# Row-maximum stage of a causal attention layer: wider units, two-bank PSUM buffers and a lead of one unit

## The reference, cut to what matters

```python
x = L0_attn_x                      # (4, 2048, 256) fp32
xn = layernorm(x)
q, k, v = split(xn @ Wqkv.T)       # 16 heads of 16
dots = (q @ k.T) * 16 ** -0.5      # per batch and head, 2048 x 2048
dots = where(causal_mask, -inf, dots)
out = softmax(dots) @ v            # softmax(z) = exp(z - max z) / sum
attn = out @ Wout.T + bout
ffn = fp4_linear(silu(fp4_linear(xn, w_gate)) * fp4_linear(xn, w_up), w_down)
return x + attn + ffn
```

## Time and profile before

| | us |
|---|---|
| runs, median of 3 | 2633.95 (2632.21 to 2635.04) |
| profiled execution | 2634.47 |
| its span | 2632.8 |
| row-maximum stage in it | 254.5 to 962.4 |
| PE busy over the span | 2336.7 (89%) |
| DVE busy over the span | 1962.6 (75%) |
| ACT busy over the span | 1956.8 (74%) |

### The profile page before, as it was taken

How to read it: one execution, slowest core, us unless ns; L and a number is a source line. 1 busy time by engine, 2 the same in 40 slices (tenths; PEclk the granted TensorE clock), 3 DMA queues, 4 the chain that set the end, 5 groups by cost and what they waited for, 6 DMA issues and landing times.

```text
span 2632.8 us, 86210 instructions
## 1 busy us (share of the span) xinstructions
PE 2336.7 (89%) x34104; PEld 1294.7 (49%) x34104; DVE 1962.6 (75%) x5676; ACT 1956.8 (74%) x3342; POOL 918.4 (35%) x780
## 2 busy tenths in 40 slices
PE   2896999999999957999999989899998999989998
PEld 1784444444444424445455545455544455554455
DVE  6675999999999975766666667576676666667665
ACT  1343999999999956787777777777777777777775
POOL 3212233333333323333333333333333433334332
PEclk7898999999999988999999999999999999999999
DMA  2576445555555513101201101201011021011000
GB/s 62 176 225 146 69 72 73 73 72 72 73 72 73 72 28 75 28 12 33 61 19 42 38 17 30 60 23 36 22 39 28 13 66 40 19 38 30 13 20 30
DMA packets 94537, 143.82 MB, mean 55 GB/s; under 512 B 24896, under 2 KB 73920, under 8 KB 93632
## 3 DMA queue, kind: packets, MB, share of 16 engines
q1 hardware_dynamic: 89792, 129.50, 25.3%
q0 software_dynamic: 4352, 8.92, 1.4%
HBM read 104.20 MB, written 34.14 MB: 53 GB/s over the span
## 4 chain that ended last, share of the span: by engine, by line
PE 35%; DVE 11%; ACT 10%; issue 7%; DMA 0%; SPq 0%; POOL 0%; DVEq 0%; ACTq 0%; POOLq 0%
PE O L1052 10%; ACT probs L1180 8%; PE F L1073 7%; PE S L1031 6%; PE F L1110 6%; PE F L1119 2%; DVE silu L1376 2%; DVE o_turned L1409 1%; PE S L1037 1%; DVE o_packed L1421 1%; PE F L1099 1%; ACT ht_hi L1198 1%; DVE gated L1380 1%; DVE o_turned L1410 1%; DVE h_amax L1331 1%
## 5 line engine op out<-in xcount | busy, mean ns | idle before, releaser
L1180 ACT ACTIVATE probs<-S 128x1024 f32<-128x1024 f32 (+3 forms) x1280 | 1081.7, 899 | 381.2 <-PE S L1031 195.1
L775 ACT ACTIVATE m_excess<-m_DIFF 128x512 f32<-128x512 f32 (+7 forms) x1536 | 646.8, 472 | 85.0 <-PE m_DIFF L735 39.8
L793 DVE CUSTOM_DVE_ANT_0 m_excess<-m_S,m_excess 128x512 f32<-128x512 f32 (+7 forms) x1536 | 700.5, 530 | 11.1 <-PE m_S L735 9.4
L1052 PE MATMUL O<-probs,v_sb 64*32 64x512 f32 (+3 forms) x10240 | 615.9, 536 | 18.5 <-DVE o_turned L1410 15.8
L1031 PE MATMUL S<-q_st,k_st 64*32 64x512 f16 (+3 forms) x10240 | 440.7, 349 | 141.9 <-ACT probs L1180 99.9
L733 PE MATMUL m_S<-m_k,m_q 128*128 128x512 f16 (+7 forms) x1536 | 482.1, 324 | 26.7 <-DVE m_row_max L793 17.4
L733 PE MATMUL m_DIFF<-m_k,m_q_diff 128*128 128x512 f16 (+7 forms) x1536 | 476.9, 318 | 26.4 <-DMA m_q_diff<-s_q 26.1
L1031 PEld LDWEIGHTS S<-q_st,k_st 64*32 64x32 f16 x10240 | 170.3, 91 | 521.4 <-ACT probs L1180 356.0
L677 POOL TENSOR_TENSOR m_q_diff<-m_zero,m_q 48x4096 f16<-48x4096 f16 x32 | 224.4, 7011 | 428.0 <-DMA m_q<-s_q 417.3
L733 PEld LDWEIGHTS m_S<-m_k,m_q 128*128 128x128 f16 x1536 | 148.0, 96 | 276.7 <-DVE m_row_max L793 195.9
L735 PE MATMUL m_S<-m_future,m_ident 128*128 128x64 bf16 x1024 | 197.0, 193 | 0.0
(11 more groups left out here) (182 smaller groups left out, 4140.8 us busy)
## 6 DMA issues: line engine op xcount, KB each, us to landing
m_q<-s_q SPq DMA_DIRECT2D x96, 128.0 KB, 3.8
m_k<-s_k SPq DMA_DIRECT2D x96, 128.0 KB, 6.8
m_q_diff<-s_q SPq DMA_DIRECT2D x96, 128.0 KB, 8.1
k_st<-s_k SPq DMA_DIRECT2D x96, 128.0 KB, 4.4
q_st<-s_q SPq DMA_DIRECT2D x384, 32.0 KB
m_k<-s_k SPq DMA_DIRECT2D x96, 124.0 KB, 5.3
a_x<-in_L_attn_x_dram POOLq DMA_DIRECT2D x16, 512.0 KB, 4.8
s_q<-a_part SPq DMA_DIRECT2D x32, 256.0 KB, 2.4
```

Of the source, the lines that this page charges most:

```text
L775: act.activation(excess[u % MAX_EXCESS][:, 0:keys // 2], DIFF[u % MAX_BUFS][:, 0:keys // 2], ACT.Relu) \
L793: dve.tensor_tensor_reduce(larger, S[u % MAX_BUFS][:, 0:keys // 2], larger, 1.0, -3e38, ALU.add, ALU.max, column).then_inc(reduced[u % MAX ...
L1052: ins = pe.matmul(O[e][s * SLOT:(s + 1) * SLOT, st.skip:QC], v_sb[st.group % 2][rows, st.j, s * SLOT:(s + 1) * SLOT], probs[s // 2][st.n % ...
L1180: act.activation(probs[half][st.n % PROBS][:, :, 0:st.width], S[half][:, :, 0:st.width], ACT.Exp, scale=scale).then_inc(exped[half], 1)
```

## The change

Query blocks are no longer cut. A unit is a whole block with up to 1024 columns, 16 units to a head instead of 24. DIFF and S have two buffers each, of two banks (1024 columns). Blocks 8 to 15 ("wide") take a buffer; blocks 0 to 7 ("narrow") lie two to a buffer, one in each bank. The order of a head's blocks, with the buffer: 15 (0), 8 (1), 7 and 0 (0), 6 and 1 (1), 14 (0), 9 (1), 13 (0), 10 (1), 5 and 2 (0), 4 and 3 (1), 12 (0), 11 (1). PE writes a wide unit with two matmuls and the mask; the number of matmuls stays the same. The semaphores are one for each kind, and a unit waits for the last one that held any of its banks (`holders`). The lead of the differences is one unit instead of two. `excess` has six buffers of 1024 columns instead of eight of 512. `second_max` and the join at the end of a round are gone.

```diff
-MAX_KEYS = 1024
-MAX_BUFS = 4
-MAX_EXCESS = 8
-MAX_LEAD = 2
+MAX_COLS = T // 2
+MAX_HALF = MAX_COLS // 2
+MAX_EXCESS = 6
+MAX_LEAD = 1
...
+class MaxUnit:
+    def __init__(self, block, buf, at):
+        self.block, self.buf, self.at = block, buf, at
+        self.cols = (block + 1) * PAIR
+        self.banks = [(buf, b) for b in range(at // MAX_HALF, (at + self.cols - 1) // MAX_HALF + 1)]
...
+    wide = [(i, i - NKB // 2) for i in range(NKB - 1, NKB - NKB // 4 - 1, -1)]
+    wide = [(i, NKB + NKB // 2 - 1 - i) for i, _ in wide]
+    narrow = [(i, NKB // 2 - 1 - i) for i in range(NKB // 2 - 1, NKB // 4 - 1, -1)]
     units = []
+    for n, pair in enumerate(wide):
+        units += [MaxUnit(i, buf, 0) for buf, i in enumerate(pair)]
+        if n % 2 == 0:
+            units += [MaxUnit(i, buf, at) for buf in range(2) for at, i in zip((0, MAX_HALF), narrow[n + buf])]
+    return units
...
+        def holders(n, u):
+            banks = set(round_units[u][1].banks)
+            for back in range(1, len(units)):
+                if before(n, u) >= back and banks & set(round_units[u - back][1].banks):
+                    return before(n, u) - back + 1
+            return 0
...
-                pe.wait_ge(exceeded[u % MAX_BUFS], uses(n, u - MAX_BUFS, MAX_BUFS) + PRIMED)
+                pe.wait_ge(exceeded, holders(n, u) + PRIMED)
...
-                pe.wait_ge(reduced[last % MAX_EXCESS], uses(n, last, MAX_EXCESS) + PRIMED)
+                pe.wait_ge(reduced, holders(n, u) + PRIMED)
...
-                    dve.tensor_tensor(row_max[:, :, split:NKB], row_max[:, :, split:NKB], second_max[:, :, :],
-                                      ALU.max).then_inc(joined, 1)
-                    dve.wait_ge(joined, n + 1 + PRIMED)
```

More of the change, by code:

```diff
@@ L580 @@
 MAX_LOAD = 2
-MAX_KEYS = 1024
-MAX_BUFS = 4
-MAX_EXCESS = 8
-MAX_LEAD = 2
+MAX_COLS = T // 2
+MAX_HALF = MAX_COLS // 2
+MAX_EXCESS = 6
+MAX_LEAD = 1
 MAX_HEADS = 8
+class MaxUnit:
[3 more added lines that the diff above has]
+        self.banks = [(buf, b) for b in range(at // MAX_HALF, (at + self.cols - 1) // MAX_HALF + 1)]
 def max_units():
+    wide = [(i, i - NKB // 2) for i in range(NKB - 1, NKB - NKB // 4 - 1, -1)]
+    wide = [(i, NKB + NKB // 2 - 1 - i) for i, _ in wide]
+    narrow = [(i, NKB // 2 - 1 - i) for i in range(NKB // 2 - 1, NKB // 4 - 1, -1)]
     units = []
[L593 to L598, removed]
+    for n, pair in enumerate(wide):
[3 more added lines that the diff above has]
+    return units
 def shift_phase(nc, once, loop_sems, ident, dram):
     units = max_units()
-    assert len(units) % MAX_EXCESS == 0 and MAX_HEADS * NKB == P
-    split = MAX_KEYS // P
+    assert sorted(unit.block for unit in units) == list(range(NKB)) and MAX_HEADS * NKB == P
     primed = []
@@ L625, in shift_phase @@
                               two("m_k", [P, MAX_LOAD, T], F16))
-        excess = [sb(f"m_excess{u}", [P, MAX_KEYS // 2]) for u in range(MAX_EXCESS)]
-        row_max, second_max = sb("m_row_max", [P, MAX_HEADS, NKB]), sb("m_second_max", [P, MAX_HEADS, NKB - split])
+        excess = [sb(f"m_excess{u}", [P, MAX_COLS]) for u in range(MAX_EXCESS)]
+        row_max = sb("m_row_max", [P, MAX_HEADS, NKB])
         row_turned, minus_max = sb("m_row_turned", [P, P]), sb("m_minus_max", [P, P])
@@ L631, in shift_phase @@
         minus_unit = sb("m_minus_unit", [P, 1])
-        S = [ctx.enter_context(nc.psum_tensor(f"m_S{u}", [P, MAX_KEYS // 2], F32)) for u in range(MAX_BUFS)]
-        DIFF = [ctx.enter_context(nc.psum_tensor(f"m_DIFF{u}", [P, MAX_KEYS // 2], F32)) for u in range(MAX_BUFS)]
+        S = [ctx.enter_context(nc.psum_tensor(f"m_S{u}", [P, MAX_COLS], F32)) for u in range(2)]
+        DIFF = [ctx.enter_context(nc.psum_tensor(f"m_DIFF{u}", [P, MAX_COLS], F32)) for u in range(2)]
         consts, zeroed, stack_ld, stack_free = once("m_consts"), [once(f"m_zeroed{p}") for p in range(2)], sems("m_stack_ld"), sems("m_stack_free")
         q_ld, q_negated = sems("m_q_ld"), sems("m_q_negated")
[L636 to L639, removed]
+        differed, exceeded, scored, reduced = sem("m_differed"), sem("m_exceeded"), sem("m_scored"), sem("m_reduced")
+        turned, negated, part0, part1, shift_st = (
+            sem("m_turned"), sem("m_negated"), sem("m_part0"), sem("m_part1"), once("m_st"))
         shift_dmas = SHIFT_PARTS * (P // SLOT)
@@ L652, in loads_before, with before @@
             return n * (loads // 2) + load // 2
-        round_units = [(h, *unit) for h in range(MAX_HEADS) for unit in units]
-        def uses(n, u, bufs):
-            return n * (len(round_units) // bufs) + u // bufs + 1
+        round_units = [(h, unit) for h in range(MAX_HEADS) for unit in units]
+        def before(n, u):
+            return n * len(round_units) + u
+        def holders(n, u):
[4 more added lines that the diff above has]
+            return 0
         @block.gpsimd
@@ L729, in _, with product @@
         def _(pe):
[L730 to L736, removed]
+            def product(out, q, h, unit, mask):
+                k = k_st[h // MAX_LOAD % 2][:, h % MAX_LOAD, :].rearrange("r (n k) -> r n k", k=P)[:, :, 0:PAIR]
+                for c0 in range(0, unit.cols, MAX_HALF):
+                    c1 = min(unit.cols, c0 + MAX_HALF)
+                    ins = pe.matmul(out[:, unit.at + c0:unit.at + c1],
+                                    q[:, h % MAX_LOAD, unit.block * P:(unit.block + 1) * P], k[:, c0 // PAIR:c1 // PAIR, :],
+                                    start=True, stop=c1 < unit.cols)
+                return pe.matmul(out[:, unit.at + unit.cols - PAIR:unit.at + unit.cols], ident_bf[:, :], mask,
+                                 start=False, stop=True)
             def differences(n, u):
-                h, i, k0, keys, _ = round_units[u]
+                h, unit = round_units[u]
                 if u % per_load == 0:
@@ L743, in differences @@
                     pe.wait_ge(q_negated[load % 2], loads_before(n, load) + 1 + PRIMED)
-                pe.wait_ge(exceeded[u % MAX_BUFS], uses(n, u - MAX_BUFS, MAX_BUFS) + PRIMED)
-                product(DIFF[u % MAX_BUFS], q_diff[h // MAX_LOAD % 2], h, i, k0, keys // 2,
-                        future[:, PAIR:P] if k0 + keys == (i + 1) * P else None).then_inc(differed[u % MAX_BUFS], 1)
+                pe.wait_ge(exceeded, holders(n, u) + PRIMED)
+                product(DIFF[unit.buf], q_diff[h // MAX_LOAD % 2], h, unit, future[:, PAIR:P]).then_inc(differed, 1)
             def scores(n, u):
-                h, i, k0, keys, _ = round_units[u]
-                last = u - MAX_BUFS
-                pe.wait_ge(reduced[last % MAX_EXCESS], uses(n, last, MAX_EXCESS) + PRIMED)
-                product(S[u % MAX_BUFS], q_st[h // MAX_LOAD % 2], h, i, k0, keys // 2,
-                        future[:, 0:PAIR] if k0 + keys == (i + 1) * P else None).then_inc(scored[u % MAX_BUFS], 1)
+                h, unit = round_units[u]
+                pe.wait_ge(reduced, holders(n, u) + PRIMED)
+                product(S[unit.buf], q_st[h // MAX_LOAD % 2], h, unit, future[:, 0:PAIR]).then_inc(scored, 1)
             pe.wait_ge(consts, 6)
@@ L770, in _ @@
                     n = b * rounds + r
[L771 to L776, removed]
+                    for u, (h, unit) in enumerate(round_units):
+                        act.wait_ge(differed, before(n, u) + 1 + PRIMED)
+                        if before(n, u) >= MAX_EXCESS:
+                            act.wait_ge(reduced, before(n, u) - MAX_EXCESS + 1 + PRIMED)
+                        act.activation(excess[before(n, u) % MAX_EXCESS][:, 0:unit.cols],
+                                       DIFF[unit.buf][:, unit.at:unit.at + unit.cols], ACT.Relu).then_inc(exceeded, 1)
         @block.vector
@@ L785, in _ @@
                     n = b * rounds + r
[L786 to L790, removed]
-                        dve.sem_inc(stack_free[h // MAX_LOAD % 2] if (u + 1) % per_load == 0 else aside, 1)
[L793 to L796, removed]
-                    dve.tensor_tensor(row_max[:, :, split:NKB], row_max[:, :, split:NKB], second_max[:, :, :],
-                                      ALU.max).then_inc(joined, 1)
-                    dve.wait_ge(joined, n + 1 + PRIMED)
+                    for u, (h, unit) in enumerate(round_units):
+                        larger = excess[before(n, u) % MAX_EXCESS][:, 0:unit.cols]
+                        dve.wait_ge(scored, before(n, u) + 1 + PRIMED)
+                        dve.wait_ge(exceeded, before(n, u) + 1 + PRIMED)
+                        dve.sem_inc(stack_free[h // MAX_LOAD % 2] if (u + 1) % per_load == 0 else aside, 1)
+                        dve.tensor_tensor_reduce(larger, S[unit.buf][:, unit.at:unit.at + unit.cols], larger, 1.0, -3e38,
+                                                 ALU.add, ALU.max, row_max[:, h, unit.block:unit.block + 1]) \
+                            .then_inc(reduced, 1)
+                    dve.wait_ge(reduced, before(n, len(round_units)) + PRIMED)
```

## The result

| | before | after |
|---|---|---|
| runs, median | 2633.08 (2632.12 to 2635.04) | 2680.57 (2680.32 to 2681.83) |
| span of the profiled execution | 2632.8 | 2678.6 |
| row-maximum stage | 707.9 | 756.9 |
| from its end to the end of the span | 1670.4 | 1666.4 |

The change made the kernel slower by 47.5 us in the median, a ratio of 1.018 (95% interval 1.0163 to 1.0198).

A forecast was written before the change was run, and what follows sets the result against it. DVE was taken to bound the row-maximum stage, hiding PE and ACT. Terms -39.9 - 2.1 + 91.5 + 0.9 - 0.7 = +49.7 us on 2634.5 gave 2684 us, range 2655 to 2705.

The forecast's parts named there:

- The saving: Row-maximum stage, DVE: 512 fewer reductions at 0.078 us each, -39.9 us, and the join gone, -2.1 us.
- The waits: Row-maximum stage: DVE stalls before blocks 14, 12, 13, 7, 11, 3, 6 and 15, 1.43 us a head, +91.5 us.
- The first two chains: DVE's stalls before block 14 (0.54 us) and block 12 (0.41 us), through PE's queue and ACT's pass.
- Small terms: DVE's shorter stalls per head: block 7 0.10 us, block 11 0.09, block 3 0.04, blocks 6 and 15 0.03 each.
- The release of DVE: Hand-off to a waiting DVE reduction: 0.22 us whoever releases; for ACT no row in the stage, lower bound 0.03.
- The first (waits stay hidden): Row-maximum stage: ACT and PE still run ahead, only the savings remain, 2593 us; chance 0.10 with what lies near.
- The second: ACT's release of DVE is quick (0.03 us): 2672 us, PE's too: 2646; far end and mixtures down to 2640: 0.10.
- The third: Row-maximum stage: PE clock falls to 1.2 GHz; a tenth of the stage so adds 35 us, 2719 us; chance 0.05.
- The fourth: The change does not do what it says; held excluded by instruction order, 128 reductions a round against 192; no chance given.
- The total: Whole kernel: +49.7 us on the profiled 2634.5, said as 2684 us, 1.9% slower.
- The 0.9 us for the start: Stage start at half clock: 2816 PE columns before the first reduction instead of 1792, +0.9 us.
- a sign of being wrong: Stages after the row maxima: the prediction counts as wrong if a later stage's length changes.

The follow-up runs named there:

- the run with the longest stage: The changed kernel with its differences two units ahead instead of one (MAX_LEAD 2 for 1): 2757.4 us, ratio 1.0469.

## Why the prediction was right, step by step

*The saving.* 0.078 us for each of 512 reductions and the join were the right price: with the waits gone the stage is 664.7 us. Against the kernel before without the increment (707.2, the like comparison) this is 42.5 less, against the kernel before itself 43.2, where the sum said 42.0.

*The waits.* The sum of 91.5 us met 91.9, and the large terms hold block by block, because each chain starts at a DVE event and is made of durations that the trace of before had. That the sum is so near is partly luck, as small errors cancelled. The first two chains were shown to be ACT's by adding work to them, and PE's order by moving the differences of two blocks. Small terms missed both ways: 11 was 0.14 in the mean and not 0.09, and blocks 6 and 15 had nearly none.

*The release of DVE.* The prediction took 0.22 us whoever releases. For PE that was measured; for ACT it is 0.17 before block 14 and 0.19 before block 12, inside the bounds given. Block 14 came out at 0.528 against 0.54 all the same, because the 0.03 us of waiting before block 6, which the sum let DVE spend meanwhile, did not occur either: the two errors nearly cancel. The reason given (the increment that goes first) is in part right: without it PE's release is 0.17 us quicker, but ACT's only 0.03, and the expectation to the run, which took 0.05 us for the increment, was too low for PE's.

*Rivals.* The first (waits stay hidden) is refuted for this order of blocks, but not for these buffers: planned otherwise they do stay hidden. The second is answered by the 0.17. The third did not come: the clock stayed at 1.00, the 2.4 GHz level, with PE busy 635 of 757 us and also in the run with the longest stage, 830.5 us. The fourth did not come either: the trace has 1024 reductions.

*The total.* 2684 was said and 2680.6 came. Up to the end of the stage 49.7 us were said, and 0.8 + 49.0 came. The 0.9 us for the start is not tested by this: in four profiles whose first instructions on PE are the same, the first reduction starts anywhere from 254.6 to 255.3 us.

The rest of the difference is what follows the stage, 1666.4 us against 1670.4. The prediction had named such a change as a sign of being wrong, and left the part as it was; its code is the same. The traces show what goes with it. Every profile has the 1.2 GHz level for the first 40 us or so behind the stage. After that the clock of the kernel before falls to it again in two short stretches of the main stage; in the changed kernel it does not. The first of them, 740 us behind the stage's end, after 699 us in which PE was busy 637:

```profile
1002.80:1702.00 699.20, 637.06 (x12273) 348.64 (x12272) 470.55 (x983) 542.52 (x759) 259.75 (x260) 1.00 0.15 33
1702.00:1710.00 8.00, 6.94 (x51) 5.19 (x50) 2.77 (x5) 2.97 (x5) 2.17 (x2) 0.57 0.61 115
```

and the same place in the changed kernel:

```profile
1752.00:1760.00 8.00, 7.32 (x103) 4.75 (x111) 5.70 (x10) 5.59 (x9) 4.70 (x5) 1.00 0.75 142
```

Over the twelve profiles of this case (the ten experiments and the two kernels), what follows the stage takes 1666.3 to 1666.5 us in the three without such stretches, 1667.4 to 1667.9 in the four where they add up to about 3 us, 1668.6 to 1669.4 in the three with about 7, and 1670.4 and 1673.0 in the two with about 10. So the prediction's reading that the clock stayed at 1.00 in the main stage was not exact; the row is rounded. No run changed the clock alone, so this is shown as an order and not as a cause, and why the clock falls there in some executions is open.

*What the profile would show.* I had said DVE busy about 663 us and 90 us of idle time before reductions. The profile says 694.7 and 72.3 (10.4 of these before the stage's first reduction): where DVE waits, an instruction's tail and its read-out count as busy that otherwise lie under the next one. From start to start the numbers agree.

## What to carry to other kernels

Larger units save a fixed cost for each on the bounding engine only while the engines before it stay hidden. With half as many buffers this was decided here by the order of the units. What worked was to let large ones follow large ones, and to issue the work of a unit ahead of any wait that stands before a run of small ones. Work such a chain out from the event that starts it to the instruction that it releases, not from busy shares: in the changed stage no engine was full on average, and yet DVE waited 92 us. When a queue is in order, a longer lead can cost more than it hides.

## What the runs showed of the hardware that was not expected

- The delay of a waiting DVE depends on the instructions that carry the wait: from PE's modelled end 0.22 us behind an event instruction that waits and increments, 0.05 us when the reduction itself waits; from ACT's end 0.17 us behind an event instruction that waits and increments, 0.14 us behind one that only waits. With DVE never waiting the same increment cost nothing (2633.6 against 2634.6 us).
- A reduction or an ACT pass over two PSUM banks had no additional cost: 1220 and 1023 ns at 1024 columns, 685 and 598 at 512; the differences, 535 and 425 ns, are those of 512 columns at the rates that the prediction read from narrower rows (columns/960 and columns/1200 us) to within 2 ns.
- The granted clock falls to the 1.2 GHz level in short stretches of the main stage in nine of twelve profiles, by up to 10 us in all, and the time of what follows the row maxima goes with it (1666.3 to 1673.0 us).
